# Token lists by three broadcast transfers, and the first expert's weights asked for one stage earlier

## What is computed

```python
gate_logits = jnp.einsum('te,ex->tx', x, gate_kernel)      # 64 experts
weights, selected = jax.lax.top_k(gate_logits, TOP_K)      # 2 of them for each token
weights = jax.nn.softmax(weights.astype(jnp.float32), axis=-1)
...                                                        # tokens sorted by expert
h0 = jax.lax.ragged_dot(sorted_x, w0, group_sizes)         # 512 -> 1024
h1 = jax.lax.ragged_dot(sorted_x, w1, group_sizes)
inter = jax.nn.silu(h0) * h1
out_sorted = jax.lax.ragged_dot(inter, wo, group_sizes)    # 1024 -> 512
...                                                        # back to tokens, weighted, added
x = x + _L1_ffn_ref(_layernorm(x, axis=-1), ...)
```

## Time and profile before

| | |
|---|---|
| Median of 3 runs | 5286.94 us (5281.24 to 5288.11) |
| The profiled execution's own time | 5282.99 us |
| Its span in the profile | 5281.0 us |
| PE busy over the span | 5001.8 us (95%) |
| DVE, ACT and POOL busy | 54%, 31% and 32% |
| The expert stage | from 3490 us to the end |
| Experts, tiles in it | 64, 164 |

### The profile page before, as it was taken

The page is one execution under the profiler, slowest core; times in us unless marked ns, Lnnn a source line. Parts: engine busy times, 40 slices in busy tenths (PEclk is TensorE's granted clock), DMA queues, the critical chain, the costliest instruction groups (busy, mean ns, idle before and its releaser), DMA issues. The chain is left out here.

```text
span 5281.0 us, 120235 instructions
## 1 busy us (share of the span) xinstructions
PE 5001.8 (95%) x46960; PEld 3484.6 (66%) x46960; DVE 2866.6 (54%) x4878; ACT 1653.9 (31%) x2074; POOL 1695.1 (32%) x1428
## 2 busy tenths in 40 slices
PE   9999989989999999899989999869999999999998
PEld 4444446668886656455444555658788999998777
DVE  4243227666654355354542565546666666666565
ACT  1001015544332200234331343213434344443333
POOL 1000005545554211000002222345444555454443
PEclk9999999989999999999999999879999999999999
DMA  1000021240111233599987111334465678889997
GB/s 59 8 32 24 8 86 37 72 109 33 24 33 48 85 127 136 140 226 212 227 178 258 54 57 55 136 107 121 120 216 174 195 250 265 273 303 347 383 383 246
DMA packets 493439, 772.00 MB, mean 146 GB/s; under 512 B 119505, under 2 KB 263638, under 8 KB 492708
## 3 DMA queue, kind: packets, MB, share of 16 engines
q1 hardware_dynamic: 377072, 723.32, 42.5%
q0 software_dynamic: 36160, 43.09, 4.1%
q10 hardware_dynamic: 79988, 2.67, 1.0%
HBM read 577.15 MB, written 116.26 MB: 131 GB/s over the span
## 5 line engine op out<-in xcount | busy, mean ns | idle before, releaser
L3474 PE MATMUL ex_ps<-ex_w,ex_xT 128*32 128x256 f32 x20992 | 1223.1, 380 | 32.0 <-DVE ex_w L3375 27.2
L3474 PEld LDWEIGHTS ex_ps<-ex_w,ex_xT 128*32 128x32 f32 x20992 | 1033.6, 110 | 168.1 <-DVE ex_w L3375 33.4
L3375 DVE COPY ex_w<-ex_shelf 128x4096 f32 x328 | 750.1, 2287 | 327.6 <-PE ex_ps L3474 167.1
L3432 ACT ACTIVATE ex_w<-ex_shelf 128x4096 f32 x164 | 594.8, 3627 | 821.3 <-PE ex_ps L3486 646.8
L3486 PE MATMUL ex_ps<-ex_w,ex_hT 128*32 128x256 f32 x10496 | 652.0, 380 | 11.1 <-ACT ex_w L3432 7.0
L3321 POOL DMA_INDIRECT ex_x<-moe_xn,ex_ix x328 | 563.2, 1717 | 136.1 <-issue 98.1
L3486 PEld LDWEIGHTS ex_ps<-ex_w,ex_hT 128*32 128x32 f32 x10496 | 524.5, 110 | 84.4 <-issue 18.5
L3338 POOL DMA_INDIRECT out<-ex_y,ex_ix_out x164 | 293.9, 1792 | 802.5 <-DVE ex_xT L3362 256.9
L2766 POOL TENSOR_TENSOR go_xb<-go_xr,go_bias 128x2048 f32<-128x2048 f32 x8 | 38.2, 4775 | 718.8 <-DMA go_xr<-x 651.8
L617 PE MATMUL at_ps<-at_xT,at_kT 128*128 128x512 f32 (+3 forms) x640 | 239.3, 529 | 1.6 <-ACT at_kT L511 1.6
L617 PEld LDWEIGHTS at_ps<-at_xT,at_kT 128*128 128x128 f32 x640 | 116.7, 190 | 121.8 <-issue 109.1
(11 more groups left out here) (358 smaller groups left out, 8030.1 us busy)
## 6 DMA issues: line engine op xcount, KB each, us to landing
ex_shelf<-L_ffn_w SPq DMA_DIRECT2D x128, 2048.0 KB
ex_shelf<-L_ffn_wo SPq DMA_DIRECT2D x64, 2048.0 KB
cv_gt<-cv_g SPq DMA_DIRECT2D x320, 128.0 KB
cv_vt<-cv_v SPq DMA_DIRECT2D x256, 128.0 KB, 5.3
ff_x<-x SPq DMA_DIRECT2D x16, 1024.0 KB
ex_raw_x<-slot_token ACTq DMA_DIRECT2D x656, 0.5 KB
at_low<-x SPq DMA_DIRECT2D x8, 1024.0 KB
x<-at_acc SPq DMA_DIRECT2D x8, 1024.0 KB, 4.2
```

Source lines behind the costliest of these rows:

```text
L3375: dve.tensor_copy(w_s[n][:, :], pick(shelf[n], buf)).then_inc(w_set[n].sem, 1)
L3432: act.activation(w_s[2][:, :], pick(shelf[2], buf), ACT.Copy).then_inc(w_set[2].sem, 1)
L3474: mm = pe.matmul(ps[r * LANES:(r + 1) * LANES, which, hh * FL:(hh + 1) * FL], xT[:, p % 2, k, hh * LANES:(hh + 1) * LANES], wu[which][:, k ...
```

## The change

Three edits.

1. `fetch` issues three transfers for a tile, not six. Each writes all 128 partitions. For `raw_x` there is one for each half of the tile's 64 pairs, whose source repeats the same 32 pairs four times (`to_broadcast([QUADS, LANES, 2])`); for `raw` the source repeats the 64 pairs twice (`to_broadcast([Q, G, 2])`). The counts that DVE waits for follow. Bytes and pieces are the same.
2. SP asks for the three weights of the first expert in the routing stage, as soon as `ex_own` is there, and the expert stage's own loads begin with the second expert.
3. DVE's `first()` in the expert stage copies w0 for tile 0 ahead of the first `turn_x`, and w1 right behind it. The third `index`, which stood ahead of both `turn_x`, comes behind the first tile's work.

```diff
@@ stage_route, block.sync
             nxt.early(sp)
+            sp.wait_ge(nxt.own_in, 16)
+            expert = nxt.entry(sp, 3 * NSLOT + 1 + NE, NE - 1)
+            for n in range(3):
+                nxt.shelve(sp, n, expert, 0)
             sp.wait_ge(spare_clear, 32)
@@ open_experts
     def fetch(act, table, base, p):
-        src = table.rearrange("(t g) c -> t g c", g=G)[bass.ds(base, 1)].rearrange("o g c -> g (o c)")
-        src_x = table.rearrange("(t h g) c -> t g h c", h=G // LANES, g=LANES)[bass.ds(base, 1)].rearrange("o g h c -> g (o h) c")
-        for a in range(QUADS):
-            act.dma_start(st.raw_x[a * LANES:(a + 1) * LANES, p], src_x).then_inc(st.raw_x_in[p], 16)
-        for q in range(Q):
-            act.dma_start(st.raw[q * G:(q + 1) * G, p, :], src).then_inc(st.raw_in[p], 16)
+        src = table.rearrange("(t g) c -> t g c", g=G)[bass.ds(base, 1)].to_broadcast([Q, G, 2])
+        for h in range(G // LANES):
+            src_x = table.rearrange("(t h g) c -> t h g c", h=G // LANES, g=LANES)[bass.ds(base, 1), h].to_broadcast([QUADS, LANES, 2])
+            act.dma_start(st.raw_x[:, p, h, :], src_x).then_inc(st.raw_x_in[p], 16)
+        act.dma_start(st.raw[:, p, :], src).then_inc(st.raw_in[p], 16)
@@ stage_experts, block.sync
-            for b in range(NBUF):
+            for b in range(1, NBUF):
                 load(b, b, None)
@@ stage_experts, block.vector
             def index(i, c, p):
-                dve.wait_ge(raw_x_in[p], i * 16 * QUADS + 16 * QUADS)
+                dve.wait_ge(raw_x_in[p], i * 16 * XH + 16 * XH)
...
             def aim(i, c, p):
-                dve.wait_ge(raw_in[p], i * 16 * Q + 16 * Q)
+                dve.wait_ge(raw_in[p], i * 16 + 16)
...
             def first():
-                for c in range(3):
+                for c in range(2):
                     index(0, c, c)
-                for c in range(2):
-                    turn_x(0, c, c)
-                for c in range(2):
-                    e, buf = owner(dve, c)
-                    for n in range(2):
-                        place(n, c, e, buf)
+                e, buf = owner(dve, 0)
+                place(0, 0, e, buf)
+                turn_x(0, 0, 0)
+                place(1, 0, e, buf)
+                index(0, 2, 2)
+                turn_x(0, 1, 1)
+                e, buf = owner(dve, 1)
+                for n in range(2):
+                    place(n, 1, e, buf)
                 gate(0, 0)
                 turn_h(0, 0)
```

## The result

| | before | after |
|---|---|---|
| median of the runs | 5288.11 us (5281.24 to 5292.89, 5 runs) | 5447.16 us (5442.14 to 5452.92, 5 runs) |
| profiled execution | 5282.99 us, span 5281.0 us | 5452.19 us, span 5450.1 us |

The ratio is 1.0308, 95% interval [1.0296, 1.0320]. The prediction's direction held; its size did not: it forecast 73 us more and at most 5430 us, and the change costs 159 us by the medians, 169 by the profiled executions. Two errors cancel in its sum, which is luck.

What follows compares the result with a forecast made beforehand. PE was taken to bound the expert stage from 3640 to 4807 us, the weights' transfers from 4807 to 5176. Start 6, middle 10 and late 57 gave +73 us on 5282.99, 5356, forecast as 5358 between two bases; range 5288 to 5430.

Steps and rivals of the forecast that it cites:

- the engines: List transfers: a small outermost source dimension puts `raw_x` on 4 engines and `raw` on 2.
- All 16 engines still carry the lists: Rival for the list transfers: no crowding, the start gains up to 9.4 us, 5276 us; chance 0.15.
- the price in engine time: Busiest engines: 101 more packets a tile at 10.6 ns, 1.07 us a tile, 34 us from 4807 to 5176.
- landings and the loss of a tile late in the stage: Late expert stage: `raw_x` lands in 14 us, or 23 behind an undrained `raw`; 13.3 us a tile, 1.8 lost.
- 1.8 x 32 = +57: Late expert stage: 1.8 us lost on each of 32 tiles, +57 us (34 to 95), engine time included.
- most fetches see 14 us: Expert stage from 3640 to 4807 us: loads come in bursts with pauses, so +10 us (0 to 60).
- the cover: DVE's index: 9.3 us of lead plus some 6.5 of slack, 15.8 in all, covers a 14 us landing, not 23.
- the estimate's 0.141: Engines under weight load: each small list packet waits for one weight piece, 0.141 us a packet.
- engine time only: Rival for the list transfers: lists wait little; 34 us late less 9 at the start, 5308 us; chance 0.22.
- A little is saved on ACT: ACT's issues: three take 2.0 us where six took about 2.9; counted as no gain in time.
- The start: Expert stage's start with early weights and new lists: PE's second tile at 3524.5 against 3518.59 us, +6 us.
- the whole gain on offer: Expert stage's start: first weights requested 9.4 us earlier, a gain kept to the end if nothing got in the way.

Runs made afterwards that it cites:

- e5: The whole change, but three list transfers from 128 different (wrong) rows each, so that 16 engines carry them: 5268.43 us, ratio 0.9978 against the kernel before.
- e4: The kernel before with only `raw` fetched by one broadcast transfer, `raw_x` by four as before: 5313.76 us, ratio 1.0058 against the kernel before.
- e7: The changed kernel, but ACT issues a tile's lists behind the silu of the same round: 5529.09 us, ratio 1.0469 against the kernel before.
- e6: The changed kernel, but `raw_x` is asked for seven tiles ahead, not four: 5519.47 us, ratio 1.0452 against the kernel before.
- e9: The changed kernel with `raw_x` asked for seven tiles ahead and both lists issued behind ACT's silu: 5479.00 us, ratio 1.0366 against the kernel before.
- e11: The changed kernel with the loop's weight loads cut to one block of 128 rows per matrix: 5247.98 us, 12 us above e10.
- e3: The kernel before with only `raw_x` fetched by two broadcast transfers, `raw` by two as before: 5418.98 us, ratio 1.0255 against the kernel before.
- e1: The changed kernel with the old six list transfers; early weights and reordered opening stay: 5282.35 us, ratio 0.9992 against the kernel before.
- e12: The kernel before plus early weights, `raw` not fetched but taken by DVE from `raw_x`, four list transfers: 5271.95 us, ratio 0.9978 against the kernel before.
- e10: The kernel before with the loop's weight loads cut to one block of 128 rows per matrix: 5235.76 us.

## Why the prediction was right in kind and wrong in size

**Right: the engines.** 4 and 2, by the packet count; e5 shows that this alone decides between +159 us and -12. The Trainium skill's rule (DMA: Bandwidth & Descriptors, Rules for kernel authors), that a small outermost dimension holds the whole transfer on so few engines, is borne out. "All 16 engines still carry the lists" fell with it, but its 5276 is near what e5 shows for a kernel in which that is so.

**Right: the price in engine time.** 10.6 ns a packet gives 25 us for e4 late in the stage, and 24.2 were measured.

**Right: landings and the loss of a tile late in the stage.** The trace doesn't name a packet's tile, so the packets of the ACT queue are counted off in order of time: when have a tile's 264 `raw_x` packets gone, from its first issue? By that count `raw_x` takes 13.9 us on average for tiles 120 to 150 and 25 us for one in ten; the forecast had 14 and 23. Before it was 6.5 us. The loss is 75.2 us in 43 tiles, 1.75 us a tile; the forecast had 1.8. That the size fits so well is in part luck: from 4878 to 5431 us PE waited 61.3 us for the copy of w0, the forecast's path, but also 20.4 us for the silu, which had no term in the forecast.

**Wrong: the number of those tiles.** "1.8 x 32 = +57" took the 32 tiles of the window to 5176 us for the whole; the stretch goes on to tile 163, 43 tiles from tile 120. At the forecast's own rate that is 77 us. This accounts for 18 to 20 us of the miss.

**Wrong: the middle, the step that failed.** "most fetches see 14 us. I take +10 us (0 to 60)": it is +84.7. By the windows above that is 53.3 us more in which PE is idle and 31.4 us in which it is busy longer for the same tiles. The forecast had no term for the second. The granted clock of 0.98 accounts for at most some 23 us of it (an estimate, 0.02 of 1154 us busy); where the rest comes from stays open. Three things were wrong in what it said of the idle time.

First, the cover. I held that an index could be 6.5 us late beyond the 9.3 us of its own lead, 15.8 us in all. Of tiles 12 to 119, 11 had their list later than 15.8 us, 39 later than 9.3, and the index waited 30 times, 149.7 us in all, between 3660 and 4878 us. Most of this was covered: PE's own wait for the copy of w0 is 20.2 us. But the slack was that of one quiet tile, and e7 shows how little there is: 2.7 us less lead cost another 82 us.

Second, bursts. The prediction knew them, but held that a backlog needs a load that lasts, and that most fetches see 14 us. By the count above they took 4.5 us in the median from tile 12 to 119 and 7.9 on average, and 18.4 in the worst: quicker than forecast between bursts, slower in them. From 4850 to 5250 us of the changed kernel the list packets go at a median of 22 a microsecond (over those in which any go), on at most 4 engines; before, from 4850 to 5150, it was 77 on 16. A quarter of the engines carries about a quarter of the rate. With 2 to 4 engines at it, 22 a microsecond is 0.09 to 0.18 us a packet on one engine, and the estimate's 0.141 lies between. An expert's weights take 16.7 us at 376 GB/s; in that time a busiest engine passes 118 list packets at 0.141 us, and 131 are asked for with each tile. So as long as a burst lasts the rate is short, in the middle as well as late, and what is left over meets the next tile's lists. This is argued from these rates; e6 and e9 agree with it: the lists are asked for three tiles earlier, and the wait turns up elsewhere.

The rival "engine time only" fell: it has lists that wait little, and late in the stage they took 13.9 us on average. The Trainium skill's other rule (DMA: Bandwidth & Descriptors, Queues, rings and completion order: an engine drains a group of some 9 to 17 descriptors from one queue, then turns to the next) was wrongly put on that rival's side, with "five weight packets, 1 us". Five such groups of weight pieces at 0.131 us each are 6 to 11 us, an estimate from that page's figure, and if both queues are served in groups of like size, the shares are as even as one for one. No run here shows the groups.

Third, ACT. "A little is saved on ACT, which isn't waited for where PE or the weights set the pace: nothing" was a term put at nothing, and it was wrong. ACT is held in the issue itself when few engines carry its lists beside the weights (e5 and e11 each take one of the two away, and in both the long issues go, but for the start of e11); that the queue of those engines is full then is inferred. PE waited 50.2 us for the silu after 3540 us, 29.8 of them in the middle, and never before the change.

What the 84.7 us would be without one of the two paths is known from one side only. Each of e6, e7 and e9 removes one wait and feeds the other. But in e3 PE never waits for the silu, and 73.7 us of loss are there all the same: late lists at the index are enough for most of it.

**The start.** Forecast +6, measured +10.7. The early request came when foretold, 0.6 us ahead of ACT's first list. What came in its place was ACT again:

```profile
3480.04 0.95 SPq L3215 DMA_DIRECT2D ex_shelf<-L_ffn_w  x2
3480.64 1.93 ACTq L3229 DMA_DIRECT2D ex_raw_x<-slot_token  x2
...
3483.36 14.04 ACTq L3229 DMA_DIRECT2D ex_raw_x<-slot_token  x2
3497.49 1.47 ACTq L3230 DMA_DIRECT2D ex_raw<-slot_token  x1
3500.98 5.29 PE L121 MATMUL ex_ps<-ex_ident 128*128 128x128 f32 x24 [28.76 <-PEq L57]
3502.23 0.23 DVE L3360 TENSOR_SCALAR ex_ix<-ex_raw_x,ex_part 128x2 uint32<-128x2 f32 x1 [26.91 <-issue]
...
3526.67 3.53 PE L3480 MATMUL ex_ps<-ex_w,ex_xT 128*32 128x256 f32 x32 [4.31 <-ACT ex_g L3443]
```

The prediction had the barrier 2 to 3 us earlier. PE's warm-up behind it starts at 3500.98, for 3490.70 us before, 10 us later, since ACT must issue the second tile's lists before it, and those two issues take 14.04 us. PE's second tile came at 3526.67; 3524.5 was forecast.

The early weights alone were put at -9.4 us and "the whole gain on offer". e1 gives -4.0 us at the start: what got in the way was the old lists, late behind the weights.

## What to carry to other kernels

Before a transfer is merged, look at the outermost dimension of its source, and count its pieces on its busiest engine against what else that engine carries in a burst; a mean DMA share below 1 says nothing of bursts. Where the rate is short, an earlier request moves the wait to whoever issues, and an issuer in whose queue compute work stands is a waiting engine like any other. The cheapest transfer is the one whose data lie on the right partition already (e12).

## What the runs showed of the hardware

- An issue on ACT's queue isn't of fixed cost. The same instruction took from 0.54 to 11.51 us (median 1.05) on 4 engines, 0.34 to 1.65 (0.39) on 16 (e5). With little other traffic beside them a tile's three issues on few engines took 2.13 us together (e11), and the six of the kernel before 2.56 (e10).
- PE's clock adds to the longer gaps. After its wait of 4.38 us the `up` at 5146.13 took 9.63 us, and one in full flow takes 7.1. The windows of that stretch (columns as above) show the granted clock at 0.50, that is 1.2 GHz, behind that gap, and back at 2.4 GHz within 6 us:

```profile
5146.00:5148.00 2.00, 1.87 (x20) 0.95 (x24) 1.97 (x4) 2.00 (x1) 0.90 (x1) 0.50 0.54 47
5148.00:5150.00 2.00, 2.00 (x28) 0.85 (x24) 2.00 (x3) 1.16 (x1) 0.00 (x0) 0.50 0.80 285
5150.00:5152.00 2.00, 2.00 (x32) 1.02 (x28) 0.75 (x4) 0.00 (x0) 1.09 (x1) 0.68 1.03 406
5152.00:5156.00 4.00, 4.00 (x80) 2.20 (x76) 2.40 (x2) 0.60 (x1) 3.44 (x2) 1.00 1.02 402
```

  At a mean of 0.93 from 4807 to 5176 us the clock alone is at most some 22 us of PE's 321 busy ones (an estimate; the mean counts idle time too), a cost that the prediction did not have.
